# Counting edges in 80 strips of 8 destinations instead of 40 windows of 16, two banks in turn

## The chip, the cores and the metric

The kernel runs on one core of one Trainium2 chip. The metric is the device time of one execution in microseconds (us). The kernel before takes 1109.0 us, the median of three runs (1108.06 to 1109.21).

The engines are named as in the profile: PE is TensorE's matrix array and PEld its weight loads, DVE is VectorE, ACT is ScalarE, POOL is GpSimd, SP issues the DMAs. A `q` behind a name (PEldq, DVEq) is the engine's sequencer, which reads the instruction stream, keeps registers, waits on semaphores and hands the work on.

## The reference

Two layers on a graph of N = 625 nodes with 1024 features and 20,000 edges (`src`, `dst`, a type from 0 to 7), edges sorted by `dst`:

```
h = x @ W;  e = exp(-leaky_relu(al[src] + ar[dst]))
h_prime = segment_sum(e * h[dst], src) / (segment_sum(e, src) + EPS)
x1 = layernorm(x + elu(h_prime))
u = x1 @ root + bias
for r in 0..7:                       # mask: edges of type r
    sums = segment_sum(x1[src] * mask, dst);  cnt = segment_sum(mask, dst)
    u = u + (sums / max(cnt, 1)) @ weight[r]
z = concat(u, x1) @ w_gate + b_gate
out = layernorm(x1 + tanh(u) * z + x1 * (1 - z))
```

All sums over edges depend only on how many edges of type r lead from node s to node d. The kernel counts them once, and every segment sum becomes a dense matrix product with the counts.

## The kernel before, in words

The edges lie in 158 tiles of 128, one edge on each partition, padded to `ALL_TILES` = 160. Because they are sorted by destination, the edges of a few neighbouring destinations lie in a few neighbouring tiles. The counts of 16 destinations (`WIN`) are made at a time, a window; there are 40 (`WINDOWS`). For a tile, DVE writes `hot` (L790): on each edge's row a one in that column, of 640, which stands for its destination in the window, its relation and its source tile. PE then multiplies (L1030) the one-hot matrix of the sources' places in their tile, `oh_s`, built once, with `hot`, and adds the product into PSUM banks 5 and 6, 320 columns each.

A window goes like this. PE and DVE each load a register from `lohi_row` (L288, in `window_range`), which holds where the window's tiles start and how many passes it needs. PE waits until ACT has copied the window before out of the banks (`window_copied`), and opens both banks with two small matmuls on zeros (L1022). Then follows a loop (`Fori`, L1023 on PE, L784 on DVE) of passes over five tiles (`BODY`). Tile s of a pass waits on PE for `built[s]`, on DVE for `counted` of the tile that used its buffer before; there are four buffers for five tiles, the fourth tile has the first tile's. 38 windows need one pass and two need two, so there are 42 passes, 210 `hot` tiles and 420 matmuls. Two more matmuls on zeros close the banks (L1035), and ACT copies the counts to `Cst` (L499), which goes to DRAM, a group of 128 destinations at a time.

Other work is woven between the windows, written out by window number, and all of it in program order on its engine. On PE: the second half of x @ W, two items of three 512-column matmuls in each of the windows 0 to 19 (L966 to L968); the turning of the counts, 16, 16 and 8 matmuls of 128 columns (L993) in windows 8, 9 and 11 of each group of eight; and later attention products (L1001 to L1003) and row sums (L1009). On DVE: the low parts of the weights and of h, dot products (L747), draining of x @ W (L747 twice and L758 in each of windows 18 to 22), and the attention scores (L766, L772, L777). On ACT: the copies and casts that belong to these.

When the last window is counted, the attention products end, and then come the relational layer (eight relations) and the gate. POOL, SP and the other engines pass from the counting on only by semaphores.

Of the kernel before, what the change touches and what calls it, by code (L numbers as in the profile page):

```python
# [5 lines left out]
def gat_rgcn_kernel(nc, dst_cols, src_cols, type_cols, dst_units, xT, x, weights, a, bias, b_gate, counts_dram, out):  # L6
    f32 = mybir.dt.float32
    f32r = mybir.dt.float32r
    bf16 = mybir.dt.bfloat16
# [17 lines left out]
    FLT_MAX = 3.4028234e38  # L27

    TILES = dst_cols.shape[1]
    BODY = 5  # L30
    SLOT = [0, 1, 2, 0, 3]
    SLOTS = 1 + max(SLOT)
    SLOT_BEFORE = [max(b for b in range(2 * BODY) if b < s + BODY and SLOT[b % BODY] == SLOT[s]) % BODY for s in range(BODY)]
    ALL_TILES = -(-TILES // BODY) * BODY
    STARTS = ALL_TILES - BODY + 1
    LOOP_END = STARTS * (ALL_TILES // BODY)
    SUB = 2
    UNITS = dst_units.shape[0]
    WIN = P // R
    WINDOWS = NP // WIN  # L40
    PER = P // WIN
    CODES = NT * R
    SPLIT = NP // 2
    NE = N + N % 2
    NCOL = [(0, 320), (320, NE - 320)]
# [14 lines left out]
    with ctx:  # L60
        def sem(name):
            return ctx.enter_context(nc.semaphore(name))

        def sb(name, shape, dt, where=ctx):
            return where.enter_context(nc.sbuf_tensor(name, shape, dt))
# [17 lines left out]
        neg_mean = sb("neg_mean", [P, NT], f32)  # L83
        dots = sb("dots", [P, 4 * NT], f32)
        key = sb("key", [P, ALL_TILES], f32)
        table = sb("table", [P, NP], f16)
        ident = ident_r[:, :].bitcast(f32)
        ones = ones_r[:, :].bitcast(f32)

        with ExitStack() as first:  # L90
            xT_raw = sb("xT_raw", [P, KT, N], f32, first)
            iota_i = sb("iota_i", [P, NP], i32, first)
            h_raw = sb("h_raw", [P, NT, H2], f32, first)
        M1 = sb("M1", [P, 2, KT, NP], f32r)
        M_lo.append(M1[:, 0, :, :])
# [5 lines left out]
            return h_parts[0:p, 2 * half + low, t, :]  # L101

        with ExitStack() as early:
            oh_s = sb("oh_s", [P, ALL_TILES * P], bf16, early)
            Cst = [None, sb("Cst1", [P, NT, R, P], f32r, early)]
            Cst[0] = sb("Cst0", [P, NT, R, P], f32r, early)
            lohi_row = sb("lohi_row", [1, WINDOWS], i32, early)
            zeros = sb("zeros", [P, P], bf16, early)
            with ExitStack() as setup:
                ints = sb("ints", [P, 3, TILES], i32, setup)  # L110
                src_tile = sb("src_tile", [P, TILES], i32, setup)
                src_in = sb("src_in", [P, TILES], i32, setup)
                src_h = sb("src_h", [P, ALL_TILES], f16, setup)
                code_f = sb("code_f", [P, TILES], f32, setup)
                iota_s = sb("iota_s", [P, P], f16, setup)
                part_col = sb("part_col", [P, 1], f32, setup)
                win_edge = sb("win_edge", [P, 2], f32, setup)
                lohi = sb("lohi", [WINDOWS, 8], f32, setup)
                units_i = sb("units_i", [UNITS, SUB * P], i32, setup)
                unit_mm = sb("unit_mm", [UNITS, 2, SUB], f32, setup)  # L120
                unit_diag = sb("unit_diag", [UNITS, 2, SUB, UNITS], f32, setup)
                iota_up = sb("iota_up", [P, SUB, UNITS], f32, setup)
                iota_down = sb("iota_down", [P, SUB, UNITS], f32, setup)
                iota_body = sb("iota_body", [P, ALL_TILES // BODY], f32, setup)
                reach = sb("reach", [WINDOWS, 2, SUB * UNITS], f32, setup)
            att16 = sb("att16", [P, NT, NP], i16, early)
            hot = sb("hot", [P, SLOTS * NP], bf16, early)
            with ExitStack() as dotting:
                a_bc = sb("a_bc", [P, 2 * D], f32, dotting)
            al_bc = sb("al_bc", [P, NP], f32, early)  # L130
            tmp = [sb(f"tmp{b}", [P, NP], f32, early) for b in range(2)]
            diag = tmp[0]
# [20 lines left out]
        def bank(b, p=P, c0=0, c=H2):  # L153
            return ps[0:p, b * H2 + c0:b * H2 + c0 + c]
# [37 lines left out]
        lohi_turned = sem("lohi_turned")  # L192
        row_done = sem("row_done")
        oh_done = sem("oh_done")
        built = [sem(f"built{s}") for s in range(BODY)]
        counted = [sem(f"counted{s}") for s in range(BODY)]
        window_counted = sem("window_counted")
        window_copied = sem("window_copied")
        turned = sem("turned")
# [67 lines left out]
        SPREAD = 20  # L267

        def items(w):
            lo, hi = [ALL * v // SPREAD for v in (w, w + 1)] if w < SPREAD else (ALL, ALL)  # L270
            return [divmod(i, NT) for i in range(lo, hi)]

        SPLIT_AT = {RING - 1: 0, RING: 2, RING + 1: 5, RING + 2: 7, RING + 3: 10}
# [2 lines left out]
        E_W, MULT_W = [], []  # L276
        for j in range(NT):
            E_W.append(max(AL_W + 2 + 2 * j, MULT_W[j - 2] + 3 if j >= 2 else 0))
            MULT_W.append(max(E_W[j] + 3, PER * j + 13))

        def hp_w(j, t):
            return MULT_W[j] + 3 + t if j < NT - 2 else WINDOWS
# [171 lines left out]
        def _(act):  # L454
# [38 lines left out]
            def copy_window(w):  # L493
                j, v = divmod(w, PER)
                act.wait_ge(window_counted, w + 1)
                if v == 0 and j >= 2:
                    act.wait_ge(flushed[j - 2], 16 * NT)
                    act.wait_ge(turned, 2 * (j - 1))
                nc.scalar.copy(Cst[j % 2][:, :, :, v * WIN:(v + 1) * WIN].rearrange("p m r d -> p (m r) d")  # L499
                               .rearrange("p (b q) d -> p b q d", b=2),  # L500
                               ps[:, 5 * H2:7 * H2].rearrange("p (b n) -> p b n", b=2)[:, :, 0:SPLIT]
                               .rearrange("p b (q d) -> p b q d", d=WIN)).then_inc(window_copied, 1)

            def copy_turned(j, part):
                m0, m1 = turn_blocks(part)
# [15 lines left out]
                act.wait_ge(att_done, j + 1)  # L521
                nc.scalar.copy(M_hi[0][:, j, :], tmp[j % 2][:, :]).then_inc(attT_hi_done, 1)

            for w in range(WINDOWS):
                copy_window(w)
                for k in range(RING - 1, KT):
                    if w == SPLIT_AT[k]:
                        split_chunk(1, k)
# [1 line left out]
                    split_chunk(SEG_Z, w - SPREAD - 1)  # L530
                for j in range(NT - 1):
                    for part in range(2):
                        if w == PER * j + 10 + 2 * part:
                            copy_turned(j, part)
                if DRAIN_FROM - 1 <= w < DRAIN_FROM - 1 + NT:
                    copy_h(1, w - DRAIN_FROM + 1)
# [121 lines left out]
        def _(dve):  # L658
# [118 lines left out]
                v.tensor_tensor(M_lo[0][:, j, :], tmp[j % 2][:, :], M_hi[0][:, j, :].bitcast(f32), ALU.subtract)\  # L777
                 .then_inc(attT_lo_done, 1)

            turn = dve.alloc_register("dve_turn")  # L780
            dve.reg_mov(turn, 0)
            for w in range(WINDOWS):
                first_pass = window_range(DVE_ENGINE, w)
                with dve.Fori(first_pass, LOOP_END, STARTS + BODY) as i:  # L784
                    dve.reg_add(turn, turn, 1)
                    n = dve.snap(turn, min_val=1, max_val=WINDOWS * ALL_TILES)
                    tile = dve.snap(i % STARTS)
                    for s in range(BODY):
                        dve.wait_ge(counted[SLOT_BEFORE[s]], n)
                        v.tensor_scalar(hot[:, SLOT[s] * NP:(SLOT[s] + 1) * NP], table[:, :], float(WIN * w),  # L790
                                        key[:, ds(tile + s, 1)], ALU.add, ALU.is_equal).then_inc(built[s], 1)
                for k in range(RING - 1, KT):
                    if w == SPLIT_AT[k] + 1:
                        split_low(1, k)
# [152 lines left out]
        @block.tensor  # L947
        def _(pe):
            mm = nc.tensor.matmul
            for s in range(BODY):  # L950
                if SLOT_BEFORE[s] >= s:
                    pe.sem_inc(counted[SLOT_BEFORE[s]], 1)

            pe.wait_ge(units_diag_done, 1)
            for c in range(2):
# [57 lines left out]

            pe.wait_ge(row_done, 1)
            pe.wait_ge(oh_done, KT)
            turn = pe.alloc_register("pe_turn")
            pe.reg_mov(turn, 0)
            for w in range(WINDOWS):
                first_pass = window_range(PE_ENGINE, w)
                pe.wait_ge(window_copied, w + 1)  # L1020
                for c in range(2):
                    mm(bank(5 + c, c=2), zeros[:, :], zeros[:, 0:2], start=True, stop=False, skip_group_check=True)  # L1022
                with pe.Fori(first_pass, LOOP_END, STARTS + BODY) as i:  # L1023
                    pe.reg_add(turn, turn, 1)
                    n = pe.snap(turn, min_val=1, max_val=WINDOWS * ALL_TILES)
                    edge = pe.snap((i % STARTS) * P)
                    for s in range(BODY):
                        pe.wait_ge(built[s], n)
                        for c in range(2):
                            last = mm(bank(5 + c, c=SPLIT), oh_s[:, ds(edge + s * P, P)],  # L1030
                                      hot[:, SLOT[s] * NP + c * SPLIT:SLOT[s] * NP + (c + 1) * SPLIT],
                                      start=False, stop=False, skip_group_check=True)
                        last.then_inc(counted[s], 1)
                for c in range(2):
                    last = mm(bank(5 + c, c=2), zeros[:, :], zeros[:, 0:2], start=False, stop=True, skip_group_check=True)  # L1035
                last.then_inc(window_counted, 1)

                for k, t in items(w):
                    xw_item(1, k, t)
                for j in range(NT - 1):  # L1040
                    for ahead, part, blocks in ((8, 0, (0, 1)), (9, 0, (2, 3)), (11, 1, (4,))):
                        if w == PER * j + ahead:
                            turn_counts(j, part, blocks)
                if w == AL_W + 1:
                    pe.wait_ge(diag_done, 1)
# [203 lines left out]
```

## Time and profile before

| | |
|---|---|
| median of 3 runs | 1109.0 us |
| the profiled execution | 1109.11 us |
| its span, first to last instruction | 1107.3 us |
| the stretch of counting, first to last count matmul | 48.4 to 201.5 us, 153.1 us |
| busy in the whole span | PE 94%, DVE 31%, ACT 25%, POOL 24% |
| mean granted clock of TensorE | 0.977 |

The profiled execution has 1.8 us outside its span. A matmul's row gives its duration to its end, and the next one starts before that, so durations of matmuls do not add up; starts do. Register and semaphore work of a sequencer isn't counted as busy, and idle time of PE that ends with it is put down to "issue".

### The profile page before, as it was taken

The page shows a single profiled execution, that of the slowest core. Times are in us where ns is not written, and L with a number is a line of the kernel's source. Part 1 is how long each engine was busy: PE and PEld are TensorE (multiplying, and loading weights), DVE is VectorE, ACT ScalarE, POOL GpSimd, SP SyncE. Part 2 cuts the span into 40 slices and gives each one's busy share as a digit, 9 for nine tenths or more (in the row PEclk, how much of TensorE's full clock was granted, in tenths as well). Part 3 has the DMA queues.
Part 4 walks back from the last instruction along what each step waited for, and adds up shares of the span by engine and source line. Part 5 has one row for each costly group of instructions (what it writes and reads, how often), then busy time and mean ns, then how long its engine had stood idle before and what let it go on. Part 6 is the DMA issues. An engine that isn't in the chain of part 4 may idle for free.

```text
span 1107.3 us, 14903 instructions
## 1 busy us (share of the span) xinstructions
PE 1042.9 (94%) x5430; PEld 857.2 (77%) x5430; DVE 344.8 (31%) x694; ACT 275.4 (25%) x470; POOL 265.8 (24%) x201
## 2 busy tenths in 40 slices
PE   5899879996999999999999999999999999999977
PEld 3566546775889889879889879889889889888855
DVE  7976765360112202202202102102102202112277
ACT  4322343383112212212212211211212211212320
POOL 0000000106331321221321321321321321327480
PEclk9999999998999999999999999999999998999989
DMA  6213335407321041041141141141141140212212
GB/s 209 76 39 108 94 96 152 133 28 262 122 76 39 30 147 37 29 146 37 31 145 38 29 146 30 38 145 34 33 146 38 30 147 28 75 48 67 76 39 92
DMA packets 63622, 91.81 MB, mean 83 GB/s; under 512 B 4116, under 2 KB 30179, under 8 KB 63429
## 3 DMA queue, kind: packets, MB, share of 16 engines
q1 hardware_dynamic: 63556, 90.86, 26.4%
q8 instruction: 51, 0.84, 0.3%
q14 instruction: 15, 0.11, 0.0%
HBM read 75.17 MB, written 15.67 MB: 82 GB/s over the span
## 4 chain that ended last, share of the span: by engine, by line
PE 84%; DVE 7%; POOL 3%; issue 3%; ACT 2%; DVEq 1%; DMA 0%; SPq 0%; ACTq 0%; POOLq 0%
PE ps L966 18%; PE ps L968 17%; PE ps L967 17%; PE ps L1154 9%; PE ps L1155 9%; PE ps L1030 4%; PE ps L993 2%; PE ps L1143 2%; DVE hot L790 2%; DVE oh_s L722 2%; POOL x_lo L426 1%; PE ps L1203 1%; POOL u L411 1%; PE ps L1205 1%; PE ps L1204 1%
## 5 line engine op out<-in xcount | busy, mean ns | idle before, releaser
L399 POOL TENSOR_TENSOR w_lo<-w_raw,w_hi 128x512 fp32r<-128x512 f32 x168 | 215.8, 1288 | 761.7 <-ACT w_hi L465 562.7
L966 PE MATMUL ps<-w_hi,M_hi 128*128 128x512 f32 (+1 forms) x560 | 223.4, 399 | 17.4 <-POOL w_lo L399 9.4
L465 ACT CAST w_hi<-w_raw 128x512 fp32r<-128x512 f32 x184 | 114.4, 622 | 498.2 <-PE ps L968 430.8
L968 PE MATMUL ps<-w_lo,M_hi 128*128 128x512 f32 (+1 forms) x560 | 219.7, 392 | 0.0
L967 PE MATMUL ps<-w_hi,M_lo 128*128 128x512 f32 (+1 forms) x560 | 219.7, 392 | 0.0
L883 DVE SCALAR_TENSOR_TENSOR u<-ps,scale,u 128x512 f32<-128x512 f32 (+1 forms) x90 | 66.4, 744 | 427.7 <-PE ps L968 427.7
L1154 PE MATMUL ps<-C_hi,x_hi 128*128 128x320 f32 (+3 forms) x640 | 194.0, 320 | 0.0
L1155 PE MATMUL ps<-C_hi,x_lo 128*128 128x320 f32 (+3 forms) x640 | 193.0, 318 | 0.0
L966 PE MATMUL ps<-w_hi,M 128*128 128x512 f32 (+1 forms) x360 | 142.9, 397 | 0.0
L967 PE MATMUL ps<-w_hi,M 128*128 128x512 f32 (+1 forms) x360 | 142.6, 396 | 0.0
L968 PE MATMUL ps<-w_lo,M 128*128 128x512 f32 (+1 forms) x360 | 142.3, 395 | 0.0
L966 PEld LDWEIGHTS ps<-w_hi,M_hi 128*128 128x128 f32 (+1 forms) x560 | 104.7, 187 | 43.5 <-POOL w_lo L399 9.9
L1154 PEld LDWEIGHTS ps<-C_hi,x_hi 128*128 128x128 f32 (+1 forms) x640 | 128.1, 200 | 0.4
L1155 PEld LDWEIGHTS ps<-C_hi,x_lo 128*128 128x128 f32 (+1 forms) x640 | 128.1, 200 | 0.4
L968 PEld LDWEIGHTS ps<-w_lo,M_hi 128*128 128x128 f32 (+1 forms) x560 | 104.6, 187 | 24.2
L967 PEld LDWEIGHTS ps<-w_hi,M_lo 128*128 128x128 f32 (+1 forms) x560 | 105.0, 187 | 22.2
L790 DVE TENSOR_SCALAR hot<-table,key 128x640 bf16<-128x640 f16 x210 | 69.6, 382 | 53.9 <-PE ps L1030 52.4
L1030 PE MATMUL ps<-hot,oh_s 128*128 128x320 bf16 x420 | 72.2, 301 | 12.4 <-DVE hot L790 5.7
L968 PEld LDWEIGHTS ps<-w_lo,M 128*128 128x128 f32 (+1 forms) x360 | 67.0, 186 | 17.5
L966 PEld LDWEIGHTS ps<-w_hi,M 128*128 128x128 f32 (+1 forms) x360 | 66.9, 186 | 16.7
L967 PEld LDWEIGHTS ps<-w_hi,M 128*128 128x128 f32 (+1 forms) x360 | 66.7, 185 | 16.6
L1030 PEld LDWEIGHTS ps<-hot,oh_s 128*128 x420 | 29.6, 97 | 43.3 <-issue 35.7
(145 smaller groups left out, 773.2 us busy)
## 6 DMA issues: line engine op xcount, KB each, us to landing
w_raw<-weights SPq DMA_DIRECT2D x192, 256.0 KB, 2.9
C_dram<-Cst SPq DMA_DIRECT2D x25, 512.0 KB, 6.0
C_hi<-C_dram SPq DMA_DIRECT2D x8, 1600.0 KB, 7.4
z<-b_gate SPq DMA_DIRECT2D x5, 512.0 KB, 9.8
u<-bias SPq DMA_DIRECT2D x5, 512.0 KB, 7.6
xT_raw<-xT SPq DMA_DIRECT2D x8, 312.5 KB, 7.5
u<-x SPq DMA_DIRECT2D x4, 512.0 KB, 5.2
out<-u SPq DMA_DIRECT2D x4, 512.0 KB
```

What stands on the lines that cost most here:

```text
L399: pool.tensor_tensor(w_lo[k % RING][:, :], w_raw[k % RING][:, :], w_hi[k % RING][:, :].bitcast(f32), ALU.subtract).then_inc(w_lo_done, 1)
L465: nc.scalar.copy(w_hi[k % RING][:, :], w_raw[k % RING][:, :]).then_inc(w_hi_done, 1)
L722: v.tensor_tensor(oh_s[:, t0 * P:t1 * P].rearrange("p (t s) -> p t s", s=P), iota_s[:, :].unsqueeze(1).broadcast_to([P, n, P]), src_h[:, t ...
L790: v.tensor_scalar(hot[:, SLOT[s] * NP:(SLOT[s] + 1) * NP], table[:, :], float(WIN * w), key[:, ds(tile + s, 1)], ALU.add, ALU.is_equal).th ...
L883: v.scalar_tensor_tensor(u[r, t, half * H2:(half + 1) * H2], bank(t, rows(t)), scale[odd][r, t:t + 1], u[r, t, half * H2:(half + 1) * H2], ...
L966: mm(o, lhs_hi[:, k, c], w_hi[k % RING][:, :], start=opens, stop=False)
L967: mm(o, lhs_lo[:, k, c], w_hi[k % RING][:, :], start=False, stop=False)
L968: last = mm(o, lhs_hi[:, k, c], w_lo[k % RING][:, :], start=False, stop=closes_)
L993: last = mm(bank(turn_bank(j, part), c0=(m - m0) * P, c=P), Cst[j % 2][:, m, r, :], ident_r[:, :], start=r == 0, stop=r == R - 1)
L1030: last = mm(bank(5 + c, c=SPLIT), oh_s[:, ds(edge + s * P, P)], hot[:, SLOT[s] * NP + c * SPLIT:SLOT[s] * NP + (c + 1) * SPLIT], start=Fal ...
L1154: mm(o, x1_hi[r, m, f], C_hi[r, m, c0:c0 + cn], start=m == 0, stop=False)
L1155: last = mm(o, x1_lo[r, m, f], C_hi[r, m, c0:c0 + cn], start=False, stop=m == NT - 1)
```

## The change

`BODY` becomes 3 and a strip has 8 destinations (`WIN` = `P // R // 2`), so there are 80 strips. `hot` has 320 columns (`HOT`) and goes into one bank: bank 5 for even strips, bank 6 for odd ones. There are two sets of three `hot` buffers, one for even and one for odd strips, with semaphores and a pass counter of their own. The opening matmuls on zeros go: the first matmul of a strip starts the bank anew. One matmul on zeros closes it. A strip waits for the copy of the strip two before it.

The first pass of a strip is written ahead of the loop, and the loop starts one pass later (`first_pass + (STARTS + BODY)`). What is woven in stands after every second strip, under the old window numbers, except the second half of x @ W, which has one item after each of the strips 0 to 39. By the inputs' destinations, 76 strips touch three tiles or fewer, and four touch more and need two passes.

```diff
-    BODY = 5
-    SLOT = [0, 1, 2, 0, 3]
+    BODY = 3
-    WIN = P // R
+    WIN = P // R // 2
+    HOT = CODES * WIN
...
-            hot = sb("hot", [P, SLOTS * NP], bf16, early)
+            hot = sb("hot", [P, 2, BODY, HOT], bf16, early)
...
+            def hots(w, i):
+                b = w % 2
+                dve.reg_add(turn[b], turn[b], 1)
+                n = dve.snap(turn[b], min_val=1, max_val=WINDOWS * ALL_TILES)
+                tile = dve.snap(i % STARTS)
+                for s in range(BODY):
+                    dve.wait_ge(counted[b][s], n)
+                    v.tensor_scalar(hot[:, b, s, :], table[:, :], float(WIN * w),
+                                    key[:, ds(tile + s, 1)], ALU.add, ALU.is_equal).then_inc(built[b][s], 1)
+
+            for half_w in range(WINDOWS):
+                first_pass = window_range(DVE_ENGINE, half_w)
+                hots(half_w, first_pass)
+                with dve.Fori(first_pass + (STARTS + BODY), LOOP_END, STARTS + BODY) as i:
+                    hots(half_w, i)
+                if half_w % 2 == 0:
+                    continue
+                w = half_w // 2
...
-                pe.wait_ge(window_copied, w + 1)
-                for c in range(2):
-                    mm(bank(5 + c, c=2), zeros[:, :], zeros[:, 0:2], start=True, stop=False, skip_group_check=True)
-                with pe.Fori(first_pass, LOOP_END, STARTS + BODY) as i:
...
+            def counts(w, i, first):
+                b = w % 2
+                pe.reg_add(turn[b], turn[b], 1)
+                n = pe.snap(turn[b], min_val=1, max_val=WINDOWS * ALL_TILES)
+                edge = pe.snap((i % STARTS) * P)
+                if first and w >= 1:
+                    pe.wait_ge(window_copied, w)
+                for s in range(BODY):
+                    pe.wait_ge(built[b][s], n)
+                    mm(bank(5 + b, c=HOT), oh_s[:, ds(edge + s * P, P)], hot[:, b, s, :],
+                       start=first and s == 0, stop=False, skip_group_check=True).then_inc(counted[b][s], 1)
+
+            for half_w in range(WINDOWS):
+                first_pass = window_range(PE_ENGINE, half_w)
+                counts(half_w, first_pass, True)
+                with pe.Fori(first_pass + (STARTS + BODY), LOOP_END, STARTS + BODY) as i:
+                    counts(half_w, i, False)
+                mm(bank(5 + half_w % 2, c=2), zeros[:, :], zeros[:, 0:2], start=False, stop=True, skip_group_check=True)\
+                    .then_inc(window_counted, 1)
```

The next rows are PE's program of one window before, with what each instruction waits for. An ISA row is a register instruction; `lohi_row` is where the start and the passes of the window are loaded from.

```order
L288 TENSOR_LOAD lohi_row
L1022 MATMUL ps<-zeros 128x2 [waits window_copied]
L1022 MATMUL ps<-zeros 128x2
L1023 UNCONDITIONAL_BRANCH
L1023 ISA
L1030 ISA [waits built0]
L1030 MATMUL ps<-hot,oh_s 128x320 x2
...
L1023 REGISTER_ALU
L1023 COMPARE_AND_BRANCH
L1035 MATMUL ps<-zeros 128x2 x2
```

And the same of one strip now:

```order
L287 TENSOR_LOAD lohi_row
L1032 ISA
L1039 ISA [waits built0_0,window_copied]
L1039 MATMUL ps<-hot,oh_s 128x320
...
L1045 ISA
L1045 UNCONDITIONAL_BRANCH
L1045 ISA
L1039 ISA [waits built0_0]
L1039 MATMUL ps<-hot,oh_s 128x320
...
L1045 REGISTER_ALU
L1045 COMPARE_AND_BRANCH
```

The pass of L1039 stands twice in a strip, once ahead of the loop and once in it. In both programs the branch ahead of the loop leads to the loop's first instruction, and the only comparison of the loop stands at its end.

DVE's program of one window before, from the register load to the end of the loop:

```order
L288 TENSOR_LOAD lohi_row
L784 UNCONDITIONAL_BRANCH
L784 ISA
L790 ISA [waits counted3]
L790 TENSOR_SCALAR hot<-table,key 128x640
...
L784 REGISTER_ALU
L784 COMPARE_AND_BRANCH
```

And of one strip now:

```order
L287 TENSOR_LOAD lohi_row
L786 ISA
L791 ISA [waits counted0_0]
L791 TENSOR_SCALAR hot<-table,key 128x320
...
L797 ISA
L797 UNCONDITIONAL_BRANCH
L797 ISA
L791 ISA [waits counted0_0]
L791 TENSOR_SCALAR hot<-table,key 128x320
...
L797 REGISTER_ALU
L797 COMPARE_AND_BRANCH
```

The pass in the loop writes the same three buffers as the pass ahead of it, and so waits for PE's matmuls of that pass.

## Rows read from the trace of the kernel before

**Rows 1.** The chain of waits that ended last, by engine.
```profile
PE 84%; DVE 7%; POOL 3%; issue 3%; ACT 2%; DVEq 1%; DMA 0%; SPq 0%; ACTq 0%; POOLq 0%
```

**Rows 2.** Stretch of counting: length, then busy time of engines, clock, DMA.
```profile
48.40:201.50 153.10, 134.55 (x928) 86.32 (x928) 98.94 (x283) 47.65 (x79) 0.15 (x1) 1.00 0.35 99
```

**Rows 3.** Timeline, one window: start, duration, engine, operation, count, idle before.
```profile
150.24 1.85 PE L1030 MATMUL ps<-hot,oh_s 128*128 128x320 bf16 x10
150.82 0.68 DVE L790 TENSOR_SCALAR hot<-table,key 128x640 bf16<-128x640 f16 x2 [0.87 <-PE ps L1030]
151.34 0.11 PEld L1030 LDWEIGHTS ps<-hot,oh_s 128*128 x2 [0.46 <-issue]
...
151.63 0.11 PEld L1030 LDWEIGHTS ps<-hot,oh_s 128*128 x2 [0.18 <-issue]
152.03 0.11 PEld L1035 LDWEIGHTS ps<-zeros 128*128 128x128 bf16 x2 [0.28 <-issue]
...
152.15 0.97 DVE L790 TENSOR_SCALAR hot<-table,key 128x640 bf16<-128x640 f16 x3
152.27 0.69 ACT L499 CAST Cst<-ps 128x640 fp32r<-128x640 f32 x1 [1.61 <-PE ps L1035]
...
153.02 0.11 PEld L1022 LDWEIGHTS ps<-zeros 128*128 128x128 bf16 x2 [0.87 <-ACT Cst L499]
...
153.40 0.11 PEld L1030 LDWEIGHTS ps<-hot,oh_s 128*128 x2 [0.27 <-issue]
```

**Rows 4.** By line: count, duration min/median/max in ns, first and last start.
```profile
L1023 PEldq FUSED_REGOPS  x42: 87/88/103, 47.0 to 197.7; - x42
...
L1023 PEldq COMPARE_BRANCH  x42: 67/67/228, 50.0 to 200.9; - x42
L1023 PEldq MOVE  x40: 29/29/38, 46.9 to 197.6; - x40
...
L288 PEldq TENSOR_LOAD <-lohi_row x40: 296/304/992, 46.4 to 196.7; - x40
...
L1030 PE MATMUL ps<-hot,oh_s x420: 296/299/308, 48.4 to 200.8; 128*128 128x320 bf16 x140
L1030 PEldq FUSED_REGOPS  x210: 46/46/114, 48.3 to 200.6; - x105
...
L790 DVEq FUSED_REGOPS  x210: 57/57/133, 44.8 to 199.9; - x105
```

**Rows 5.** Groups by shape on DVE, 48 to 201 us: busy, mean ns.
```profile
L790 DVE TENSOR_SCALAR hot<-table,key 128x640 bf16<-128x640 f16 x210 | 69.6, 382 | 53.9 <-PE ps L1030 52.4 <-issue 1.4
...
L812 DVE TENSOR_SCALAR tmp<-ident,alr 128x128 f32<-128x128 f32 x5 | 1.1, 281 | 0.0
```

**Rows 6.** Timeline, the end of another window.
```profile
147.98 0.11 PEld L1030 LDWEIGHTS ps<-hot,oh_s 128*128 x2 [0.18 <-issue]
148.22 0.15 PEld L1035 LDWEIGHTS ps<-zeros 128*128 128x128 bf16 x2
```

**Rows 7.** Timeline on PE, two items of x @ W between windows.
```profile
62.59 0.47 PE L966 MATMUL ps<-w_hi,M_hi 128*128 128x512 f32 x1
...
64.07 0.20 PE L1022 MATMUL ps<-zeros 128*128 128x2 bf16 x2
```

**Rows 8.** Timeline on PE, 16 turning matmuls.
```profile
148.36 1.97 PE L993 MATMUL ps<-ident,Cst 128*128 128x128 f32 x16
```

**Rows 9.** Timeline on DVE, draining x @ W between two windows.
```profile
125.03 0.69 DVE L747 SCALAR_TENSOR_TENSOR M_lo<-ps,a_bc 128x512 fp32r<-128x512 f32 x1
...
126.85 0.97 DVE L790 TENSOR_SCALAR hot<-table,key 128x640 bf16<-128x640 f16 x3
```

**Rows 10.** Stretches as in rows 2; the clock is third from the end.
```profile
130.60:134.20 3.60, 1.95 (x14) 0.87 (x14) 3.40 (x11) 1.36 (x4) 0.00 (x0) 1.00 0.02 7
...
255.50:265.00 9.50, 0.07 (x2) 0.02 (x1) 0.00 (x0) 2.75 (x5) 9.50 (x6) 0.76 0.63 208
265.00:270.00 5.00, 5.00 (x12) 3.94 (x13) 0.00 (x0) 0.00 (x0) 3.63 (x3) 0.50 0.54 164
```

More of the change, by code:

```diff
@@ L29, in gat_rgcn_kernel @@
     TILES = dst_cols.shape[1]
-    BODY = 5
-    SLOT = [0, 1, 2, 0, 3]
-    SLOTS = 1 + max(SLOT)
-    SLOT_BEFORE = [max(b for b in range(2 * BODY) if b < s + BODY and SLOT[b % BODY] == SLOT[s]) % BODY for s in range(BODY)]
+    BODY = 3
     ALL_TILES = -(-TILES // BODY) * BODY
@@ L38, in gat_rgcn_kernel @@
     UNITS = dst_units.shape[0]
-    WIN = P // R
+    WIN = P // R // 2
     WINDOWS = NP // WIN
     PER = P // WIN
+    PAIRS = PER // 2
     CODES = NT * R
+    HOT = CODES * WIN
     SPLIT = NP // 2
@@ L85, in gat_rgcn_kernel @@
         key = sb("key", [P, ALL_TILES], f32)
-        table = sb("table", [P, NP], f16)
+        table = sb("table", [P, HOT], f16)
         ident = ident_r[:, :].bitcast(f32)
@@ L91, in gat_rgcn_kernel @@
             xT_raw = sb("xT_raw", [P, KT, N], f32, first)
-            iota_i = sb("iota_i", [P, NP], i32, first)
+            iota_i = sb("iota_i", [P, HOT], i32, first)
             h_raw = sb("h_raw", [P, NT, H2], f32, first)
@@ L103, in gat_rgcn_kernel @@
         with ExitStack() as early:
[L104 removed]
+            oh_s = sb("oh_s", [P, NT * R * RING * P], bf16, early)
             Cst = [None, sb("Cst1", [P, NT, R, P], f32r, early)]
@@ L194, in gat_rgcn_kernel @@
         oh_done = sem("oh_done")
-        built = [sem(f"built{s}") for s in range(BODY)]
-        counted = [sem(f"counted{s}") for s in range(BODY)]
+        built = [[sem(f"built{b}_{s}") for s in range(BODY)] for b in range(2)]
+        counted = [[sem(f"counted{b}_{s}") for s in range(BODY)] for b in range(2)]
         window_counted = sem("window_counted")
@@ L269, in items @@
         def items(w):
-            lo, hi = [ALL * v // SPREAD for v in (w, w + 1)] if w < SPREAD else (ALL, ALL)
+            lo, hi = [ALL * v // (2 * SPREAD) for v in (w, w + 1)] if w < 2 * SPREAD else (ALL, ALL)
             return [divmod(i, NT) for i in range(lo, hi)]
@@ L278, in gat_rgcn_kernel @@
             E_W.append(max(AL_W + 2 + 2 * j, MULT_W[j - 2] + 3 if j >= 2 else 0))
-            MULT_W.append(max(E_W[j] + 3, PER * j + 13))
+            MULT_W.append(max(E_W[j] + 3, PAIRS * j + 13))
         def hp_w(j, t):
@@ L498, in copy_window @@
                     act.wait_ge(turned, 2 * (j - 1))
[L499 to L502, printed above, removed]
+                nc.scalar.copy(Cst[j % 2][:, :, :, v * WIN:(v + 1) * WIN].rearrange("p m r d -> p (m r) d"),
+                               bank(5 + w % 2, c=HOT).rearrange("p (q d) -> p q d", d=WIN)).then_inc(window_copied, 1)
             def copy_turned(j, part):
@@ L522, in att_high @@
                 nc.scalar.copy(M_hi[0][:, j, :], tmp[j % 2][:, :]).then_inc(attT_hi_done, 1)
-            for w in range(WINDOWS):
-                copy_window(w)
+            for half_w in range(WINDOWS):
+                copy_window(half_w)
+                if half_w % 2 == 0:
+                    continue
+                w = half_w // 2
                 for k in range(RING - 1, KT):
@@ L532, in _ @@
                     for part in range(2):
-                        if w == PER * j + 10 + 2 * part:
+                        if w == PAIRS * j + 10 + 2 * part:
                             copy_turned(j, part)
@@ L778, in att_low @@
                  .then_inc(attT_lo_done, 1)
[L780 to L791, printed above, removed]
+            turn = [dve.alloc_register(f"dve_turn{b}") for b in range(2)]
+            for b in range(2):
+                dve.reg_mov(turn[b], 0)
+            def hots(w, i):
[12 more added lines that the diff above has]
+                    hots(half_w, i)
+                if half_w % 2 == 0:
+                    continue
+                w = half_w // 2
                 for k in range(RING - 1, KT):
@@ L949, in _ @@
             mm = nc.tensor.matmul
-            for s in range(BODY):
-                if SLOT_BEFORE[s] >= s:
-                    pe.sem_inc(counted[SLOT_BEFORE[s]], 1)
+            for b in range(2):
+                for s in range(BODY):
+                    pe.sem_inc(counted[b][s], 1)
             pe.wait_ge(units_diag_done, 1)
@@ L1015, in _ @@
             pe.wait_ge(oh_done, KT)
[L1016 to L1019, printed above, removed]
-                pe.wait_ge(window_copied, w + 1)
-                for c in range(2):
-                    mm(bank(5 + c, c=2), zeros[:, :], zeros[:, 0:2], start=True, stop=False, skip_group_check=True)
-                with pe.Fori(first_pass, LOOP_END, STARTS + BODY) as i:
[L1024 to L1038, printed above, removed]
@@ new lines, in _ @@
+            turn = [pe.alloc_register(f"pe_turn{b}") for b in range(2)]
+            for b in range(2):
+                pe.reg_mov(turn[b], 0)
+            def counts(w, i, first):
[5 more added lines that the diff above has]
+                    pe.wait_ge(window_copied, w)
+                for s in range(BODY):
+                    pe.wait_ge(built[b][s], n)
+                    mm(bank(5 + b, c=HOT), oh_s[:, ds(edge + s * P, P)], hot[:, b, s, :],
+                       start=first and s == 0, stop=False, skip_group_check=True).then_inc(counted[b][s], 1)
@@ new lines, in _ @@
+            for half_w in range(WINDOWS):
+                first_pass = window_range(PE_ENGINE, half_w)
[4 more added lines that the diff above has]
+                    .then_inc(window_counted, 1)
+                for k, t in items(half_w):
@@ L1039, in _ @@
                     xw_item(1, k, t)
+                if half_w % 2 == 0:
+                    continue
+                w = half_w // 2
                 for j in range(NT - 1):
                     for ahead, part, blocks in ((8, 0, (0, 1)), (9, 0, (2, 3)), (11, 1, (4,))):
-                        if w == PER * j + ahead:
+                        if w == PAIRS * j + ahead:
                             turn_counts(j, part, blocks)
```

## The prediction, as put on record before the changed kernel ran

> **What bounds the kernel now.** I read the chain of waits first. It lies on PE for 84% [rows 1]. Then I looked at the one stretch that the change touches, in which 42 passes of counting are made: 48.4 to 201.5 us, 153.1 us long, at the full clock [rows 2]. Behind it everything hangs on semaphores from the counting and its woven work, so I take the rest as shifted, and neither stretched nor shortened.
>
> In that stretch neither PE nor DVE is full: DVE is busy for 99 of 153 us [rows 2]. A window is a ring of waits, and the timeline shows its links [rows 3]. Ten count matmuls start at 150.24. The fourth tile needs the first tile's buffer: DVE starts at 150.82 and PE's load for it follows at 151.34. The bank is closed at 152.03, ACT copies it from 152.27 for 0.69 us, and PE opens the next window at 153.02, 0.05 us after the copy. First count to first count that is 153.40 - 150.24 = 3.2 us, where the copy and its two semaphores are about 1.0 us and the buffer stall some 0.3 us. The change removes both from the ring: a second bank, and a set of buffers for each.
>
> **Does a strip run one pass or two?** This decides everything. In the program of now the pass stands twice in a strip, ahead of the loop and in it, and the only comparison is at the loop's end; what stands in front is a branch to the loop's first instruction. The trace bears out that nothing is tested on the way in: the loop's register instruction and its comparison ran 42 times each, as often as there were passes, and its start was set 40 times [rows 4]. A test at the entrance would have left 40 comparisons more. Before, every window had at least one pass, so that was harmless. Now the loop starts with the second pass, and 76 of 80 strips have no second pass. They run it nevertheless, over the three tiles behind theirs, which hold no edge of the strip and add zeros. The four strips with two passes run two. So I count 160 passes: 480 `hot` tiles instead of 210, and 480 matmuls of 320 columns instead of 420.
>
> **One strip, step by step,** from its first count matmul at 0. The buffers of the second pass are those of the first, so the second pass is again a round trip between the engines:
> - The first matmul ends at 0.30 [rows 4]. In the window of before the second matmul of the first tile starts 0.135 behind 150.24 (320 columns at full clock and a little), ends at 150.67, and DVE starts at 150.82: 0.15.
> - `hot` is 382 ns for 640 16-bit columns, 1280 bytes, and 281 ns for 512 bytes [rows 5]. On the line through these two, 640 bytes take 298 ns. The bounds are 281 and 382. I take 0.30.
> - From `hot` ready (150.82 + 0.38 = 151.20) to PE's load (151.34) 0.14 [rows 3]. Both first tiles of a pass have a longer register instruction, 114 against 46 ns and 133 against 57 at most [rows 4]; I add 0.05 for each. Round trip: 0.30 + 0.15 + 0.30 + 0.14 + 0.10 = 1.0.
> - Two further tiles at DVE's pace. Two `hot` take 0.68, so a second one adds 0.30 to 0.38 [rows 3]; with 0.08 less each it is 0.21: 0.42.
> - From the last tile's load to the closing load 0.24 [rows 6] to 0.40 [rows 3]: 0.28.
> - Then the register load, 0.30 [rows 4], and register work to the next count, which before was 153.40 - 153.02 = 0.38 [rows 3], with 0.04 to start it: 0.72. Before, the load ran under ACT's copy. Now there is no copy to wait for and nothing hides it.
> - Sum 2.42 us. DVE's own way to the next strip's first `hot` is a little shorter by the same steps, so PE's sequencer ends last. ACT is not in the ring: it has two strips for its copy, and even if a 320-column copy were as long as one of 640, 0.69 us, it would be done.
>
> Eighty strips are 193.6 us. With every step at its low end (no longer register instructions, closing 0.24, 0.66 for the load) a strip is 2.2, with `hot` at the old pace (0.38 and twice 0.30) and closing at 0.40 it is 2.8.
>
> **Work that doesn't fit between.** After the closing matmul PE has 0.7 us free while its sequencer is at its registers. One item of x @ W is half of 64.07 - 62.59 = 1.48, so 0.74 [rows 7], and just fits. The turning of 16 blocks takes about 1.78 of array time (1.97 with the last one's end) [rows 8]. In the four windows with x @ W it is added whole, in the four later ones less 0.7; the groups of 8 add 0.9 twice and 0.2 twice: 7.1 + 4.3 + 1.8 + 0.4 = 13.6. The attention products, six of 512 columns at 0.23 and in six windows, add 0.66 four times and 1.37 twice, the row sums 1.1 three times, at the pace of rows 8, the broadcast of al 1.3: 9.9 in all. DVE has about 0.8 us of the same kind, between the last `hot` of a strip and the time at which PE can use the next: its sequencer is at its registers meanwhile. I size it by PE's 0.7, as both do the same steps. A single operation of 0.6 to 0.75 hides there. A drain takes 126.85 - 125.03 = 1.82 [rows 9] and adds 1.0, five times; pairs of operations add 0.4 to 0.7 in some seven windows: 8.4. Together 32 us, between 22 and 40, since I can't see how these overlap.
>
> **The sum.** 193.6 + 32 = 225.6 instead of 153.1: +72.5. Against the profiled execution, 1109.1 (span 1107.3 and 1.8 around it; it stands 0.1 above the median), that gives 1181.6. The ACT copies, 80 instead of 40, and fewer matmuls on zeros cost nothing here; the setup is the same but for arrays half as wide, and its cover is the first half of x @ W, which ends just ahead of the first window's register work at 47.0 [rows 4].
>
> What would the skill say? Of `hot`, where two rows give a fixed part under half the width, the Trainium skill (VectorE: DVE Perf Modes, the section on the TRN2 errata) says that operations reading SBUF pay a fixed extra per instruction, and that "many small tiles pay it per-tile". The trace agrees: 281 ns for two fifths of the bytes that take 382. Without such a part 640 bytes would take 0.19, the two further tiles 0.15 each, and a strip 2.42 - 0.11 - 0.12 = 2.19 us, the time 1163. By the rule and the rows it is 1182.
>
> **Rivals.**
> 1. The loop runs only where a second pass is due. Then a strip is one pass: from the first to the third matmul 0.27, to the close 0.28, 0.72 to the next: 1.3 us, so 104 us, and 5 for the four second passes. With all 32 us of woven work that is 141; where buffers built a strip ahead hide much of it, near 109. I take 120, a third of the way: 1109.1 - 33 = 1076, or up to 1097. For it: DVE and PE truly have slack. Against it: the counts in rows 4 and the order. 3%.
> 2. The sequencers do more side by side than I add up: PE's register load starts while the count matmuls still run, and woven work hides wholly. 80 x 2.2 + 22 = 198, +45: 1154. It would need the closing matmul not to wait behind the comparison, while in rows 3 it does. 12%.
> 3. The clock falls. In a strip without x @ W, PE has six matmuls of 0.133 in 2.42 us, a third. The granted clock fell to the lower level (1.2 GHz, 0.50) only when PE had done next to nothing for 9.5 us; a stretch with 14 short matmuls in 3.6 us kept 1.00 [rows 10]. At the lower level every matmul is 0.13 longer, some three of them in the ring, 0.4 x 40 strips = 16 us: 1198. 5%. The Trainium skill (TensorE: Matmul & The Clock Gate, Part 1) says that activity releases the throttle and idleness brings it back; the trace agrees for long idleness, and by that rule a sparser stage is the one to watch.
> 4. DVE ends last: `hot` stays near 382 ns and its register load comes behind waits that PE's closing delays. 80 x 2.7 + 32 = 248, +95: 1204. The 281 ns row speaks against it. 12%.
>
> My forecast, two passes at 2.3 to 2.55 a strip, has 68%: 80 times -0.12 and +0.13 around the sum, and some us for the woven work, 1169 to 1196. The range for 8 in 10 is 1157 to 1204. About 0.2%, 2.2 us, can be told from no change here. Slower by more has the forecast and rivals 2 to 4, 97%; faster has most of rival 1, 2.5%; no change 0.5%.
>
> **What would show it.** In the profile after: 480 count matmuls and 480 `hot`, loop comparisons 80, not 4; `hot` at about 298 ns; PE idle put down to "issue" and to DVE in each strip; no wait of PE for ACT's copy; the stage some 225 us long and the clock at 1.00 in it; later stretches as long as before. I am wrong if the comparisons number 4 or the matmuls 252, if a plain strip is under 2.2 or over 2.7 us, or if the time behind the stage changes.

## The result, and the profile after

The changed kernel takes 1211.8 us (median of four runs, 1210.8 to 1213.4), the kernel before 1108.5 on the same chip: a ratio of 1.093, 95% interval 1.091 to 1.095. It became slower, as forecast, but by 103 us where 72.5 were forecast, and the time lies outside the range of 1157 to 1204.

The profiled execution has a span of 1209.3 us. Here are its stretches: the counting, its first 40 and its last 40 strips, the rest, and the first 11.6 us of the rest (columns as in rows 2).

```profile
48.30:302.40 254.10, 200.40 (x909) 114.01 (x910) 147.54 (x553) 53.94 (x118) 0.00 (x0) 0.78 0.20 60
48.30:159.80 111.50, 89.83 (x470) 50.71 (x470) 71.13 (x275) 22.60 (x52) 0.00 (x0) 1.00 0.23 66
159.80:302.40 142.60, 110.57 (x442) 63.30 (x442) 76.41 (x279) 31.34 (x66) 0.00 (x0) 0.61 0.18 56
302.40:1209.30 906.90, 876.89 (x4376) 748.24 (x4375) 204.87 (x347) 209.78 (x365) 263.79 (x191) 0.97 0.24 77
...
302.40:314.00 11.60, 11.06 (x47) 10.40 (x47) 1.45 (x2) 2.64 (x5) 5.06 (x4) 0.50 0.78 228
```

And the same two of before, behind the counting:

```profile
201.50:1107.30 905.80, 876.23 (x4374) 747.23 (x4374) 204.33 (x346) 210.16 (x365) 263.74 (x191) 0.97 0.24 77
...
201.50:213.00 11.50, 10.96 (x73) 9.95 (x74) 1.65 (x2) 2.71 (x5) 4.83 (x4) 1.00 0.82 229
```

The counting grew from 153.1 [rows 2] to 254.1 us, by 101; behind it the kernel is as long as before to about a microsecond. The clock column, third from the end, holds the surprise: 1.00 in the first 40 strips, 0.61 in the last 40, and still 0.50 in the 11.6 us after them, in which PE got through 47 matmuls where it had done 73 before.

Now the rows by line that answer to rows 4 and 5:

```profile
L1045 PEldq FUSED_REGOPS  x160: 72/78/88, 48.7 to 300.9; - x160
L1045 PEldq ALU_OP  x80: 36/36/42, 49.7 to 302.1; - x80
L1045 PEldq COMPARE_BRANCH  x80: 67/67/97, 49.8 to 302.2; - x80
...
L1039 PE MATMUL ps<-hot,oh_s x480: 298/308/491, 48.3 to 302.2; 128*128 128x320 bf16 x160
...
L791 DVE TENSOR_SCALAR hot<-table,key x480: 284/298/305, 47.9 to 301.7; 128x320 bf16<-128x320 f16 x160
```

There are 80 comparisons, 480 count matmuls and 480 `hot`: every strip runs two passes. And `hot` takes 298 ns, the value read off the line through two other shapes.

One sign needs a look. The profile puts 15 of PE's waits in this stage, 8.6 us in all, down to ACT's copy. The copies that it names, such as the one from 230.40 to 230.82 ahead of the count matmul at 230.82, are of the strip just closed, which this program doesn't wait for. The copy that it does wait for, of the strip before that one, ended at 228.17. So the forecast's "no wait of PE for ACT's copy" stands.

One strip of the first half, on the timeline (columns as in rows 3):

```profile
63.89 0.58 PE L1039 MATMUL ps<-hot,oh_s 128*128 128x320 bf16 x3
64.39 0.73 DVE L791 TENSOR_SCALAR hot<-table,key 128x320 bf16<-128x320 f16 x3 [0.38 <-PE ps L1039]
...
64.89 0.68 PE L1039 MATMUL ps<-hot,oh_s 128*128 128x320 bf16 x3 [0.42 <-DVE hot L791]
...
65.50 0.17 PE L1047 MATMUL ps<-zeros 128*128 128x2 bf16 x1
...
66.31 0.45 PE L1039 MATMUL ps<-hot,oh_s 128*128 128x320 bf16 x2
```

From 63.89 the first pass, at 64.39 DVE begins to write its buffers again for the second, at 64.89 PE counts them: the round trip is 1.00 us. The close is at 65.50, 0.61 later, and the next strip's first count at 66.31. That is 2.42 us.

And one strip of the last 40, with the products woven in behind it:

```profile
236.85 0.98 PE L1039 MATMUL ps<-hot,oh_s 128*128 128x320 bf16 x3 [0.46 <-DVE hot L791]
238.00 0.98 PE L1039 MATMUL ps<-hot,oh_s 128*128 128x320 bf16 x3 [0.16 <-DVE hot L791]
238.77 0.21 PE L1047 MATMUL ps<-zeros 128*128 128x2 bf16 x1
...
239.41 0.63 PE L1012 MATMUL ps<-M,M_lo 128*128 128x512 f32 x1
239.84 0.63 PE L1013 MATMUL ps<-M,M_hi 128*128 128x512 f32 x1
```

The round trip is 1.15 us now, three count matmuls take 0.98 us instead of 0.58 (first pass) and 0.68 (second), and the attention products start 0.43 apart instead of 0.23: PE is at the lower level, 1.2 GHz.

### The profile page after: what moved, and what is told of

Its sections match the earlier page's. It is cut to its first block, busy times and chain, and to the rows that moved or that the text cites. A ratio compares the mean times of both kernels' runs of the same rounds, so it can differ in the third digit from the quotient of the medians.

```text
span 1209.3 us, 16344 instructions
## 1 busy us (share of the span) xinstructions
PE 1110.1 (92%) x5410; PEld 887.0 (73%) x5410; DVE 393.8 (33%) x964; ACT 281.3 (23%) x510; POOL 265.4 (22%) x201
## 4 chain that ended last, share of the span: by engine, by line
PE 81%; DVE 7%; issue 4%; POOL 3%; ACT 2%; DVEq 2%; DMA 0%; POOLq 0%; SPq 0%; ACTq 0%
PE ps L976 16%; PE ps L977 16%; PE ps L978 16%; PE ps L1169 8%; PE ps L1170 8%; PE ps L1039 6%; PE ps L1003 3%; DVE hot L791 2%; PE ps L1158 2%; DVE oh_s L722 1%; POOL x_lo L425 1%; POOL u L410 1%; POOL M_lo L403 1%; DVEq L791 1%; PE ps L1011 1%
## 5 line engine op out<-in xcount | busy, mean ns | idle before, releaser
L1039 PE MATMUL ps<-hot,oh_s 128*128 128x320 bf16 x480 | 122.7, 365 | 54.6 <-DVE hot L791 44.7
L791 DVE TENSOR_SCALAR hot<-table,key 128x320 bf16<-128x320 f16 x480 | 118.5, 299 | 106.0 <-PE ps L1039 76.5
L1039 PEld LDWEIGHTS ps<-hot,oh_s 128*128 x480 | 47.4, 102 | 124.0 <-issue 106.2
L498 ACT CAST Cst<-ps 128x320 fp32r<-128x320 f32 x80 | 34.1, 426 | 200.1 <-PE ps L1047 200.1
L977 PEld LDWEIGHTS ps<-w_hi,M 128*128 128x128 f32 (+1 forms) x360 | 66.8, 186 | 16.8
```

The lines of the kernel that those rows point to most:

```text
L791: v.tensor_scalar(hot[:, b, s, :], table[:, :], float(WIN * w), key[:, ds(tile + s, 1)], ALU.add, ALU.is_equal).then_inc(built[b][s], 1)
L977: mm(o, lhs_lo[:, k, c], w_hi[k % RING][:, :], start=False, stop=False)
L1039: mm(bank(5 + b, c=HOT), oh_s[:, ds(edge + s * P, P)], hot[:, b, s, :], start=first and s == 0, stop=False, skip_group_check=True).then_in ...
```

## The experiments

All times are medians; each ratio is to the kernel before on the same chip, with its 95% interval.

**The loop alone, taken back.** `e1_plain` is the changed kernel with all passes in the loop.

```diff
-                hots(half_w, first_pass)
-                with dve.Fori(first_pass + (STARTS + BODY), LOOP_END, STARTS + BODY) as i:
+                with dve.Fori(first_pass, LOOP_END, STARTS + BODY) as i:
                     hots(half_w, i)
...
-                counts(half_w, first_pass, True)
-                with pe.Fori(first_pass + (STARTS + BODY), LOOP_END, STARTS + BODY) as i:
-                    counts(half_w, i, False)
+                if half_w >= 1:
+                    pe.wait_ge(window_copied, half_w)
+                mm(bank(5 + half_w % 2, c=2), zeros[:, :], zeros[:, 0:2], start=True, stop=False, skip_group_check=True)
+                with pe.Fori(first_pass, LOOP_END, STARTS + BODY) as i:
+                    counts(half_w, i)
```

> The changed kernel, but the loop holds every pass, as in the kernel before (no pass ahead of it; a matmul on zeros opens the bank). Theory (the second pass is empty and costs a round trip, and the sparse stage loses the clock): 84 comparisons, 252 count matmuls and 252 hot; the round trip of 1.0 us and two further tiles of 0.2 go from 76 strips, a plain strip takes 1.3 to 1.4 us, the clock stays at 1.00 in the stage; time 1065 to 1095. Rival (the cost lies in 80 register loads and loop entries, whatever the passes are): the time stays over 1150.

1088.3 us, ratio 0.981 (0.977 to 0.985); run again as `e12_plain_again`:

> e1_plain again, to compare with e11_spread on the same chip and to narrow its interval against the kernel before: 1085 to 1094, ratio 0.977 to 0.986.

1090.5 us, 0.984 (0.981 to 0.987). The stage is 138.0 us long:

```profile
47.90:185.90 138.00, 124.99 (x760) 84.80 (x761) 91.23 (x325) 53.30 (x118) 0.00 (x0) 0.90 0.36 110
```

So the tiling by itself, two banks and two sets, makes the kernel faster by 1.6 to 1.9%. The way the loop is written costs 116 of the stage's 254 us, what it loses of the clock included. A plain strip (one without woven work beyond an item of x @ W) takes 1.31 to 1.36 us in the first half, where the item and the three count matmuls fill PE's array: it is busy for 6.00 of the 6.00 us from 60 to 66.

**The loop alone, put in.** `e10_peeled` is the kernel before, with one pass ahead of the loop, on PE and DVE alike, and nothing else.

```diff
-                with pe.Fori(first_pass, LOOP_END, STARTS + BODY) as i:
+                counts(first_pass)
+                with pe.Fori(first_pass + (STARTS + BODY), LOOP_END, STARTS + BODY) as i:
+                    counts(i)
```

> The kernel before (40 windows of 16, one pair of banks) with only the change in how the loop is written: one pass ahead of it, and the loop from the second pass on. Theory (a loop's body runs at least once, so 38 windows get an empty pass): 80 passes, 400 hot and 800 count matmuls; the windows with two passes took 2.4 us more than their neighbours before, so 38 x 2.4 = 91 us, time about 1198, between 1185 and 1210. Rival (the empty pass comes of the new tiling, not of the loop's form): 1105 to 1110.

1196.0 us, 1.080 (1.076 to 1.083): +89, where 91 was expected from two windows of the trace of before. Loop comparisons: 40; count matmuls: 800. From both sides the cause of the second pass is the loop's form. And in this kernel, where a window with its empty pass has 20 count matmuls in 5.6 us, the clock nearly held; it was at its lower level three times between 176 and 193 us, 10 us in all:

```profile
48.60:291.50 242.90, 203.62 (x1308) 111.10 (x1308) 161.57 (x473) 47.38 (x77) 0.00 (x0) 0.98 0.22 63
```

**The clock.** `e2_warm` gives PE more to do in the strips 40 to 79 of the changed kernel.

```diff
+                for _ in range(0 if w < 40 else 2 if first else 3):
+                    mm(bank(5 + b, c=HOT), zeros[:, :], oh_s[:, 0:HOT], start=False, stop=False, skip_group_check=True)
```

> The changed kernel with more matmuls: in the strips 40 to 79 two matmuls of zeros by 320 columns behind the first pass and three behind the second, which add nothing to the counts and lie where PE waits or has only register work. Theory (from 167 us on the lower clock costs some 27 us, because PE does too little): the clock stays at 1.00, the strips 40 to 79 take 115 to 120 us instead of 140, time 1188 to 1198. Rival (the later strips are longer because of DVE's and ACT's woven work, not of the clock): 1212 or more, since PE only has more to do.

1186.7 us, 1.070 (1.066 to 1.075). With 200 matmuls more it is 25 us faster than the changed kernel (0.0229 of 1107), a little more than expected. Its last 40 strips, and the first 11.7 us behind them:

```profile
160.60:284.30 123.70, 100.81 (x642) 61.98 (x642) 74.95 (x279) 31.40 (x66) 0.00 (x0) 1.00 0.21 64
...
284.30:296.00 11.70, 11.18 (x76) 9.98 (x75) 1.94 (x3) 2.65 (x5) 4.97 (x4) 1.00 0.78 225
```

Those strips take 123.7 instead of 142.6 us at a clock of 1.00 instead of 0.61, and the stretch behind them has its 76 matmuls again. PE's long pauses are there in both kernels, the longest from 178.84 to 180.87 us in the changed one and from 179.10 to 180.83 here, and here they did not bring the clock down: it is the work between them that differs. The two profiles differ by 18 us in the counting and 6 behind it, the latter less firmly: what follows the counting took 897 to 908 us in the profiles of this study. The extra matmuls may cost something themselves where woven work fills PE; then the clock's price is higher than 18 and 25, and no run shows by how much.

The clock was not steady ahead of them either: in `e2_warm` it was low from 157.6 to 161.0 us, in strips that still had their items of x @ W and no added matmuls, where the changed kernel, with the same program up to there, kept it until 167.3.

`e9_plain_warm` does the like to `e1_plain` (`for _ in range(3 if half_w >= 40 else 0)`, behind the passes).

> As e1_plain, with three matmuls of zeros by 320 columns behind the passes of the strips 40 to 79; they add nothing. Theory (e1_plain loses the clock for 28 us of the later strips, since PE is too sparse there): the clock stays at 1.00 in the stage, and 28 us of half speed turn into some 20: 4 to 10 us faster than e1_plain, less what the extra 0.4 us a strip cost where they show. Rival (PE's speed doesn't matter there): as e1_plain or slower by up to 10 us.

1090.0 us, 0.986 (0.983 to 0.990): no gain. The clock was 1.00 in the whole stage instead of 0.90, and yet the stage was 138.5 instead of 137.9 us, from the first to the last start of a count matmul. The strips show both sides: one of 6.60 us, with its woven work at the lower clock, takes 3.91, and the five of 0.46 take 0.86 to 0.99. With one pass a strip the extra matmuls stand in the way about as much as the clock gives back.

**The round trip or the work?** `e8_third` runs both passes, with a third set of buffers, and semaphores and a pass counter of its own, for the pass in the loop.

```diff
-            hot = sb("hot", [P, 2, BODY, HOT], bf16, early)
+            hot = sb("hot", [P, 3, BODY, HOT], bf16, early)
...
-                b = w % 2
+                b = w % 2 if first else 2
```

> The changed kernel with a third set of three buffers, which the pass in the loop uses; both passes still run. Theory (the second pass costs by the round trip of 1.0 us between PE and DVE, more than by its work): DVE builds the second pass without waiting for the first; a strip is then as long as DVE's sequencer needs for two passes, about 2.0 us instead of 2.43, 25 to 40 us faster than the changed kernel, and PE's denser work gives back some of the low clock. Rival (the work of the extra pass alone is the cost): within 5 us of the changed kernel.

1138.1 us, 1.031 (1.027 to 1.035): 69 us faster than the changed kernel by the ratios, twice what I expected. A plain strip:

```profile
66.45 1.27 PE L1039 MATMUL ps<-hot,oh_s 128*128 128x320 bf16 x6
66.90 1.49 DVE L791 TENSOR_SCALAR hot<-table,key 128x320 bf16<-128x320 f16 x6
67.67 0.17 PE L1047 MATMUL ps<-zeros 128*128 128x2 bf16 x1
...
68.47 1.27 PE L1039 MATMUL ps<-hot,oh_s 128*128 128x320 bf16 x6
```

It takes 68.47 - 66.45 = 2.02 us, as expected: six tiles in one run, no round trip. 80 x 0.4 = 32 us is that. The other 37 come on top. Part of it is the clock, 0.93 over the stage against 0.78. The rest shows where the clock plays no part: up to the first count of strip 40 both kernels have it at 1.00, and there `e8_third` takes 90.2 us and the changed kernel 113.4, so 23 us less and 0.58 a strip, not 0.4. Some strips beside woven work gain more than plain ones, up to 1.2 us; that DVE, free of those waits, builds ahead beside that work would explain it, but wasn't tried.

**The second bank.** `e3_onewait` is `e1_plain` with `pe.wait_ge(window_copied, half_w + 1)`, the copy of the strip just before.

> As e1_plain, but each strip waits for the copy of the strip before it, as the windows of before do, though the banks still take turns. Theory (the second bank takes a copy of 0.43 us and its semaphores out of the ring, but only where no item of x @ W stands between two strips): nothing in the strips 0 to 39, about 0.5 us in some 30 of the later ones, 10 to 20 us above e1_plain. Rival (the second bank is worth nothing, since registers and woven work cover the copy): within 4 us of e1_plain.

1128.2 us, 1.019 (1.015 to 1.023): 40 us above `e1_plain`, where I expected 10 to 20. The first half's plain strips take 1.59 us instead of 1.34, where I had expected nothing. In the second half:

```profile
197.11 0.21 PE L1045 MATMUL ps<-zeros 128*128 128x2 bf16 x1
197.87 0.18 PE L1042 MATMUL ps<-zeros 128*128 128x2 bf16 x1 [0.55 <-ACT Cst L498]
198.26 0.58 PE L1036 MATMUL ps<-hot,oh_s 128*128 128x320 bf16 x3 [0.21 <-issue]
```

From the close to the next first count 1.15 us, of which the wait for the copy is the larger part; and the clock was 0.79 over the stage, with three count matmuls in a strip of 1.6 to 1.9 us. To the first count of strip 40 it takes 75.2 us instead of `e1_plain`'s 67.8, both at 1.00, and from there 98.3 instead of 70.1. Plain strips of the second half take 1.56 us at the full clock and 1.91 at the lower one, so part of those 28 us is the clock again: a wait that makes PE sparse is paid twice. The shares weren't taken apart.

**The buffer stall of before.** `e6_slots` is the kernel before with

```diff
-    SLOT = [0, 1, 2, 0, 3]
+    SLOT = [0, 1, 2, 3, 0]
```

> The kernel before with SLOT = [0, 1, 2, 3, 0]: the fifth tile of a pass has the first tile's buffer instead of the fourth. Theory (in each window PE stands still for about 0.3 us until DVE has rebuilt the first tile's buffer for the fourth): the rebuild falls beside the fourth tile's matmuls, 0.2 to 0.3 us less in each of 42 passes, 8 to 12 us faster than before. Rival (the next window's first tile is now built later and takes the wait over): no change.

1094.7 us, 0.990 (0.986 to 0.994), 11 us faster: the 0.3 us stall of each window, seen in rows 3, in one line.

```profile
145.28 1.57 PE L1030 MATMUL ps<-hot,oh_s 128*128 128x320 bf16 x10 [0.18 <-issue]
```

Ten matmuls take 1.57 us instead of 1.85 [rows 3].

**What ends last in `e1_plain`?** Three tries. `e4_early` loads the next strip's register ahead of this strip's passes, on both engines.

```diff
-                first_pass = window_range(PE_ENGINE, half_w)
+                first_pass, ahead_p = ahead_p, window_range(PE_ENGINE, min(half_w + 1, WINDOWS - 1))
```

> As e1_plain, and PE and DVE load the register of the next strip ahead of the passes of this one. Theory (one pass a strip, then the sequencers' registers end last): the load of 0.30 us no longer stands between two strips on either sequencer; up to 0.35 us less for each strip in which nothing else ends last, 10 to 28 us under e1_plain. Rival (PE's array work and DVE's operations fill the stage by then): within 5 us of e1_plain.

1091.8 us, 0.986 (0.982 to 0.991): nothing. Plain strips are as long as in `e1_plain` in both halves. Where x @ W fills PE's array the load was hidden. Elsewhere I take it that the sequencer spends its 0.30 us wherever the load stands; that is argued from these strips and not shown.

`e5_body4` has passes of four tiles (`BODY = 4`).

> As e1_plain with passes of four tiles and two sets of four buffers: 80 passes instead of 84, 320 count matmuls and 320 hot instead of 252. Theory: a fourth tile adds 0.12 us of PE's sequencer and 0.21 of DVE to each strip, and four second passes of 1.2 us go: 4 to 12 us above e1_plain. Rival (a pass costs by its waits, not by its tiles): a few us under e1_plain.

1090.4 us, 0.985 (0.981 to 0.988). Plain strips are 1.47 us instead of 1.34, as expected, and the stage is 3 us longer; the time, for which 4 to 12 us more were expected, can't be told from `e1_plain`'s.

`e11_spread` has the turning matmuls in blocks of 8, one block a strip.

> As e1_plain, with each group's turning matmuls spread over both strips of a pair, one block of 8 a strip, instead of 16 behind every second. Theory (a strip with 16 turning matmuls takes 3.0 us and its neighbour 1.3, which is the sequencer's floor; 8 beside 0.85 us of idle array hide in part): 4 to 10 us faster than e1_plain. Rival (PE's array is the floor in these strips): within 2 us of e1_plain.

1090.2 us, 0.984 (0.981 to 0.987), against 1090.5 of `e12_plain_again` beside it: no difference, as the rival had it. Two strips of 2.1 us stand where one of 3.0 and one of 1.26 stood.

So `e1_plain` beats both kernels; none of the variants improves on it. It is also what rival 1 of the prediction described, with 1076 us and 1097 at most; it comes to 1088 to 1091.

## Why the prediction was wrong

**Two passes a strip: right.** There are 80 comparisons and 480 matmuls after, and both experiments on the loop's form bear it out. The start of the loop set 40 times and its comparison run 42 times [rows 4], beside the order, were enough to see it.

**A plain strip of 2.42 us: right,** in the round trip, 1.00, by its parts. The exact total has some luck in it: two tiles and the close took 0.61 where the sum had 0.70, and the rest 0.81 where it had 0.72. Whole strips of 2.42 to 2.44 us are the usual ones in the first half.

**Woven work of 32 us: up to 10 short.** With the clock held (`e2_warm`) the stage is 236.0 us. Less 80 x 2.43 = 194.4 that leaves 42, just above the range of 22 to 40. A part of it may be the added matmuls where PE was full; no run separates them. Alone this would have made 1192, inside the forecast.

**The clock: the step that failed.** The sum had nothing for it; I gave its fall 5% as a rival and priced it at 16 us. It fell at 167.3 us and was low for 111 of the stage's 254 us. The last item of x @ W starts at 159.8. Between it and the fall lie eight turning matmuls and only two strips without an item, at 161.74 and 164.18, each with six count matmuls; the fall itself lies in a pause of PE behind them, 165.97 to 167.74. So it didn't take a long row of sparse strips. That the clock stayed low through most of the stage is their doing: `e2_warm` has the pauses too, and more work in the strips keeps the clock.

My reason was twofold, and neither half carries it. The row of 14 matmuls in 3.6 us at 1.00 [rows 10] is one short stretch between fuller ones, in a kernel whose windows had ten count matmuls in 3.1 us. And I wrote that the clock fell only when PE had done next to nothing for 9.5 us. The mean of 0.76 in that row says that it fell inside the stretch, not behind it. Above all, the trace of before has falls without idleness, behind the row sums of the relational layer (columns as in rows 2, and one row of the timeline):

```profile
335.80 2.85 PE L1143 MATMUL ps<-ones_r,C_hi 128*128 128x2 f32 x25
...
335.80:338.50 2.70, 2.70 (x26) 2.70 (x25) 0.00 (x0) 0.62 (x1) 1.27 (x1) 1.00 0.28 91
...
339.00:342.40 3.40, 3.40 (x15) 3.40 (x14) 0.87 (x3) 0.43 (x1) 0.00 (x0) 0.50 0.32 82
```

PE is busy for all of that time by the profile, with 25 matmuls of 2 columns, and 0.3 us behind them the clock falls. There are eight such blocks, and seven have a fall in them or within 1.4 us behind, at 339, 421, 506, 588, 673, 755 and 919 us. A busy share doesn't tell how much PE's array has to do, and this stood in the trace before the change ran.

The Trainium skill (TensorE: Matmul & The Clock Gate, Part 1) says that activity releases the throttle and that idleness brings it back, and I had named it as the rule to watch. `e2_warm`, whose added work kept the clock up, agrees with the first half. The rows go further than the second: in the changed kernel's stage PE was never idle for longer than 2.0 us, and in the rows above not at all.

The price was short too. I had counted three matmuls in the ring of each of 40 strips. In a plain strip the low clock costs less than that, 0.15 to 0.2 us, but it nearly doubles all that is woven in, 0.43 instead of 0.23 for a product. By the profiles the stage is 28.5 us longer than the forecast's 225.6: 18 for the clock (254.1 against `e2_warm`'s 236.0) and 10 for the woven work. What lies behind the stage adds 1.1 (906.9 against 905.8), which makes 1181.6 + 28.5 + 1.1 = 1211.2; the profiled execution took 1211.1. By the times of whole runs the clock is worth 25, and the 6 us between the two figures lie behind the stage, where the clock stayed low for 11.6 us more but the profiles also differ without that. Even with the rival's 16 us in the sum it would have come to 1198, 14 short.

## What to carry to other kernels

A loop whose body runs at least once makes a pass ahead of it cost a whole pass wherever it was meant to run none; count the loop's comparisons against the passes in the trace. A producer and a consumer that share one set of buffers pay a round trip for each pass, here 1.0 us for 0.4 us of matmuls. When a change makes PE's work in a stage sparser, a lower clock for that stage is a case to price in full, with all the matmuls woven in and behind it. To see whether it is likely, look through the trace for every stretch with a lower clock and at what PE did ahead of it, not at idle time alone. A few matmuls of zeros in gaps that exist anyway can test it; in one kernel here they paid 25 us, in the other nothing.

## What the runs showed of the hardware that I had not expected

The granted clock was at its lower level for 111 us of the stage although PE never paused for longer than 2.0 us: in strips of 2.4 us PE had six matmuls of 320 columns. 200 added matmuls on zeros made that kernel 25 us faster. In the kernel before it fell in or just behind seven of eight blocks of 25 two-column matmuls, in which PE shows no idle time. A register load from SBUF took 0.30 us of PE's sequencer [rows 4], and moving it earlier (`e4_early`) saved nothing.
